# Attention in stages of a quarter of the queries, with maxima 29 units ahead instead of 40

## The reference

```
Q, K, V = (heads(WQ), heads(WK), heads(WV))
score = jnp.einsum('bhqd,bhkd->bhqk', Q, K) / jnp.sqrt(jnp.asarray(D_K, x.dtype))
score = score + mask
score = score - jnp.max(score, axis=-1, keepdims=True)
score = jnp.exp(score)
score = score / jnp.sum(score, axis=-1, keepdims=True)
out = jnp.einsum('bhqk,bhkd->bhqd', score, V)
```

## Time and profile before

| | us |
|---|---|
| median of 3 runs | 620.17 (620.04 to 621.65) |
| profiled execution | 619.71 |
| its span | 617.9 |
| PE busy | 571.0 (92%) |
| DVE busy | 475.7 (77%) |
| ACT busy | 330.8 (54%) |
| POOL busy | 191.1 (31%) |

### The profile page before, as it was taken

The page is one execution under the profiler, slowest core; times in us unless marked ns, Lnnn a source line. Parts: engine busy times, 40 slices in busy tenths (PEclk is TensorE's granted clock), DMA queues, the critical chain, the costliest instruction groups (busy, mean ns, idle before and its releaser), DMA issues.

```text
span 617.9 us, 11935 instructions
## 1 busy us (share of the span) xinstructions
PE 571.0 (92%) x3875; PEld 353.1 (57%) x3902; DVE 475.7 (77%) x1307; ACT 330.8 (54%) x602; POOL 191.1 (31%) x221
## 2 busy tenths in 40 slices
PE   2878999999999999999999988988899999999996
PEld 1433544444454534999999953444446666656554
DVE  6799889999989898455555579657689899976465
ACT  2752667676777676655555468753232642262224
POOL 1450000000254452133333311000007686688400
PEclk9798899999999999999999999998899999999999
DMA  8945727060813271111111043124010322421322
GB/s 196 234 145 204 243 73 216 2 215 2 224 42 100 67 210 32 44 49 47 47 47 47 25 130 90 70 70 120 0 46 15 90 63 59 123 87 40 103 68 68
DMA packets 55611, 57.99 MB, mean 94 GB/s; under 512 B 8650, under 2 KB 39402, under 8 KB 55514
## 3 DMA queue, kind: packets, MB, share of 16 engines
q1 hardware_dynamic: 51242, 50.56, 29.2%
q0 software_dynamic: 4320, 6.81, 3.5%
HBM read 41.96 MB, written 18.85 MB: 98 GB/s over the span
## 4 chain that ended last, share of the span: by engine, by line
PE 72%; DVE 17%; ACT 4%; issue 4%; DMA 1%; SPq 1%; ACTq 0%; DVEq 0%
PE banks L1690 11%; PE banks L1832 9%; PE banks L1963 7%; PE banks L1779 6%; PE banks L1757 6%; PE banks L1702 6%; DVE banks L1240 5%; PE banks L1952 5%; PE banks L1949 5%; PE banks L2014 4%; DVE mpart L1243 3%; ACT arena L809 2%; PE banks L1651 2%; PE banks L1760 2%; PE banks L1599 1%
## 5 line engine op out<-in xcount | busy, mean ns | idle before, releaser
L809 ACT ACTIVATE arena<-banks 128x512 f32<-128x512 f32 (+1 forms) x304 | 154.3, 583 | 75.2 <-PE banks L1760 40.7
L1240 DVE CUSTOM_DVE_ANT_0 banks<-banks,arena 128x512 f32<-128x512 f32 (+3 forms) x256 | 119.8, 511 | 9.3 <-PE banks L1779 8.4
L1779 PE MATMUL banks<-arena 96*128 96x512 bf16 (+3 forms) x384 | 113.5, 336 | 7.0 <-DVE mpart L1240 3.2
L1757 PE MATMUL banks<-arena 128*128 128x512 bf16 (+3 forms) x358 | 106.5, 327 | 3.9 <-ACT arena L809 3.3
L1243 DVE TENSOR_REDUCE mpart<-banks 128x1 f32<-128x512 f32 x128 | 85.8, 684 | 9.1 <-PE banks L1779 8.0
L1690 PE MATMUL banks<-arena 128*128 128x128 f32 x624 | 76.3, 275 | 1.0 <-ACT arena L743 1.0
L1690 PEld LDWEIGHTS banks<-arena 128*128 128x128 f32 x624 | 72.8, 192 | 1.5 <-ACT arena L743 1.5
L1832 PE MATMUL banks<-arena 128*9 128x512 f32 (+3 forms) x768 | 70.7, 487 | 0.0
L852 ACT ACTIVATE arena<-banks 125x512 f32<-125x512 f32 (+2 forms) x48 | 28.4, 595 | 71.2 <-PE banks L1949 46.2
L1757 PEld LDWEIGHTS banks<-arena 128*128 128x128 bf16 x384 | 37.8, 99 | 49.5 <-issue 23.6
L620 POOL DMA_INDIRECT results<-arena x39 | 37.7, 967 | 77.4 <-DVE arena L1134 77.4
(11 more groups left out here) (295 smaller groups left out, 868.3 us busy)
## 6 DMA issues: line engine op xcount, KB each, us to landing
k_parts<-arena SPq DMA_DIRECT2D x6, 768.0 KB, 7.4
arena<-in_L_ffn_experts_w_dram SPq DMA_DIRECT2D x2, 2048.0 KB, 11.0
arena<-results SPq DMA_DIRECT2D x8, 512.0 KB, 6.8
arena<-k_parts SPq DMA_DIRECT2D x7, 576.0 KB
arena<-q_parts SPq DMA_DIRECT2D x28, 144.0 KB
arena<-in_L_ffn_w_kernel_dram SPq DMA_DIRECT2D x8, 344.0 KB, 3.6
slots<-in_pad_rows_dram SPq DMA_DIRECT2D x1, 2535.0 KB, 12.1
arena<-slots SPq DMA_DIRECT2D x39, 65.0 KB, 1.8
```

The lines of the kernel that those rows point to most:

```text
L809: act.activation(Pr[:, r % 4, heads[0]:heads[-1] + 1, 0:n], ring_e[e % 3][:, 0:len(heads) * n].rearrange("p (j c) -> p j c", j=len(heads)) ...
L1240: ins = dve.tensor_tensor_reduce(unmasked, unmasked, tail_mask[:, 512 - n:512], 1.0, -BIG, ALU.add, ALU.max, part[:, at:at + 1])
L1757: ins = pe.matmul(ring_e[e % 3][:, at * n:at * n + n], QK[:, slot, j, 1, P * kt:P * kt + P], QK[:, slot, j, 0, q:q + n], start=True, stop= ...
L1779: ins = pe.matmul(ps[:, at * n:at * n + n], QK[0:TALL, slot, j, 0, P * i:P * i + P], QK[0:TALL, slot, j, 1, 512 * half:512 * half + n], st ...
```

## The change

- Stages are now a quarter of the queries (256) and one key tile: 20 stages and 36 exponential units a group. `Pr` holds eight narrow stages instead of four wide ones.
- Value matmuls come in six bursts of two to four stages. There are four "evac" copies a group, each of 256 columns.
- Maxima are finished by quarter: four "negmax" and four turns a group. Tiles go in the order (1, 0), (3, 2), (5, 4), (7, 6). Row (g, c) is now the row of quarter c. A turn is two matmuls instead of four, with 128 standing columns instead of 12; the buffer `MP` is wider for it and is filled with zeros at the start.
- 12 units come before the first exponential, then two for each exponential until the lead is 29 units, then 38 for 36 exponentials.
- The experts come at stage 4 of group 6. 225 exponential units and 266 maxima units then stand ahead of them, where it was 239 and 279; 63 and 38 stand behind, where it was 65 and 25.
- SyncE's list follows the plan: each row where its turn stands, loads for the group after next behind a group's fourth row. The vectors, the expert blocks and now also the experts' results are at the experts' step, so ahead of row (6, 3). The second sequence's parts are stored behind row (0, 2) instead of (0, 0).
- On ScalarE two copies of K and Q parts move from ahead of the first exponential to ahead of the fifth.

```diff
-STAGES = [(half, kt) for half in range(2) for kt in range(QT // 2 * half + QT // 2)]
+QW, NQ = 256, 4
+STAGES = [(c, kt) for c in range(NQ) for kt in range(2 * c + 2)]
 NS = len(STAGES)
+LAST_STAGE = [2, 6, 12, 20]
+BURSTS = {4: (0, 1), 7: (2, 3, 4, 5), 10: (6, 7, 8), 13: (9, 10, 11), 17: (12, 13, 14, 15)}
...
-SCATTER_AT, SCATTER_EVERY = 3 * EXP_UNITS + 20, 3
-EXPERTS_AT = (6, 3)
+SCATTER_AT, SCATTER_EVERY = 3 * EXP_UNITS + 14, 3
+EXPERTS_AT = (6, 4)
...
-MAX_TILES = ((3, 0, 2, 1), (7, 4, 6, 5))
-OPENING, LEAD, ROW_DELAY, POOL_DELAY = 22, 40, 3, 6
+MAX_TILES = ((1, 0), (3, 2), (5, 4), (7, 6))
+MAX_UNITS = sum(len(max_steps(0, i)) for i in range(QT))
+OPENING, LEAD, ROW_DELAY, POOL_DELAY = 12, 29, 3, 6
+ON_VECTOR = ((0, 0), (0, 1))
+PARTS_AT = 4
...
-            for i in MAX_TILES[half]:
+        for c in range(NQ):
+            for i in MAX_TILES[c]:
                 for step in max_steps(g, i):
                     count(step)
-            steps.append(("negmax", g, half))
-            due.append([ROW_DELAY if g + half == 0 else POOL_DELAY, ("maxrow", g, half)])
+            steps.append(("negmax", g, c))
+            due.append([ROW_DELAY if (g, c) in ON_VECTOR else POOL_DELAY, ("maxrow", g, c)])
...
-                plan += maxima(OPENING + (LEAD + half0 - OPENING) * n // half0 if n < half0 else n + LEAD)
+                plan += maxima(min(OPENING + 2 * n, LEAD + n * MAX_UNITS // EXP_UNITS))
...
+    if r == 1:
+        return [("pv", k - 1, stage) for stage in range(NS - 4, NS)] + [("evac", k - 1, NQ - 1)] if k > 0 else []
+    if k == NG or r not in BURSTS:
         return []
-    if r == 1:
-        return [("pv", k - 1, NS - 2), ("pv", k - 1, NS - 1), ("evac", k - 1, 1)] if k > 0 else []
-    if k == NG:
-        return []
-    return [("pv", k, r - 3), ("pv", k, r - 2)] + ([("evac", k, 0)] if r - 2 == QT // 2 - 1 else [])
+    steps = [("pv", k, stage) for stage in BURSTS[r]]
+    return steps + [("evac", k, c) for c in range(NQ) if LAST_STAGE[c] == BURSTS[r][-1] + 1]
...
-        Pr = region(12288, 8192).rearrange("p (s j t) -> p s j t", s=4, j=HG)
+        Pr = region(12288, 8192).rearrange("p (s j t) -> p s j t", s=8, j=HG)
...
-        MP = region(24832, 2 * QT * 3 * HG // 2, BF16).rearrange("p (s i c) -> p s i c", s=2, i=QT)
+        MP = region(24832, 1024, BF16).rearrange("p (s i c) -> p s i c", s=2, i=QT)
...
-            for g in range(NG):
-
-                if g == EXPERTS_AT[0] + 1:
+            def blocks_and_vectors():
...
-                if g == 0:
-                    sp.wait_ge(Z["rows_in"], 16 * 9)
-                for half in range(2):
-                    sp.wait_ge(Z["mrow_ready"], 2 * g + half + 1)
-                    sp.dma_start(QK[TALL:TALL + 3, g % 3, :, 0, 512 * half:512 * half + 512],
-                                 mrow[0:3 * HG, g % 2, 512 * half:512 * half + 512]).then_inc(mrow_in[half], 16)
-                    if (g, half) == (EXPERTS_AT[0] + 1, 0):
-                        load_results()
-                    elif (g, half) == (0, 0):
-                        store_parts(1)
+                    load_results()
+
+            def rows_in_place(g, c):
+                sp.wait_ge(Z["mrow_ready"], NQ * g + c + 1)
+                sp.dma_start(QK[TALL:TALL + 3, g % 3, :, 0, QW * c:QW * c + QW],
+                             mrow[0:3 * HG, g % 2, QW * c:QW * c + QW]).then_inc(mrow_in[c], 16)
+
+            def loads_behind(g):
...
+            sp.wait_ge(Z["rows_in"], 16 * 9)
+            for k in range(-1, NG + 1):
+                for step in PLANS[k]:
+                    if step[0] == "maxrow":
+                        _, g, c = step
+                        rows_in_place(g, c)
+                        if (g, c) == (0, 2):
+                            store_parts(1)
+                        if c == NQ - 1:
+                            loads_behind(g)
+                    elif step[0] == "experts0":
+                        blocks_and_vectors()
...
+            pool.memset(MP, 0.0).then_inc(Z["mem_set"], 1)
...
+            def second_copies(c):
+                for v in (2 * c, 2 * c + 1):
+                    act.wait_ge(Z["r1_done"], v - 3)
+                    act.copy(parts1[v % 2][:, 1, 512 * (c - 2):512 * (c - 2) + 512], rem1[:, v - 4, :]).then_inc(Z["p2_done"], 1)
...
+                        if e == PARTS_AT:
+                            second_copies(3)
                         act.wait_ge(Z["e_ready"], e + 1)
-                        if r >= 4:
-                            act.wait_ge(Z["pv_done"], r - 3)
-                        act.activation(Pr[:, r % 4, heads[0]:heads[-1] + 1, 0:n],
+                        if r >= 8:
...
-                        pe.wait_ge(Z["mp_ready"], 2 * g + half + 1)
+                        _, g, c = step
+                        pe.wait_ge(Z["mp_ready"], NQ * g + c + 1)
+                        pe.wait_ge(Z["mem_set"], 2)
                         ps = unit_free()
-                        for i in range(4):
-                            ins = pe.matmul(ps[0:3 * HG, P * i:P * i + P], MP[:, g % 2, 4 * half + i, :], ident_b, start=True, stop=True)
+                        for i in range(2):
+                            ins = pe.matmul(ps[:, P * i:P * i + P], MP[:, g % 2, 2 * c + i, :], ident_b, start=True, stop=True)
                         ins.then_inc(Z["m_ready"], 1)
```

More of the change, by code:

```diff
@@ L65, in heads_of @@
     return tuple(range(HG)) if j == 0 else ()
-STAGES = [(half, kt) for half in range(2) for kt in range(QT // 2 * half + QT // 2)]
+QW, NQ = 256, 4
+STAGES = [(c, kt) for c in range(NQ) for kt in range(2 * c + 2)]
 NS = len(STAGES)
+LAST_STAGE = [2, 6, 12, 20]
+BURSTS = {4: (0, 1), 7: (2, 3, 4, 5), 10: (6, 7, 8), 13: (9, 10, 11), 17: (12, 13, 14, 15)}
 def exp_steps(stage):
-    half, kt = STAGES[stage]
-    heads = [heads_of(j, 512 - max(0, P * kt - 512 * half)) for j in range(HG)]
+    c, kt = STAGES[stage]
+    heads = [heads_of(j, QW - max(0, P * kt - QW * c)) for j in range(HG)]
     return [("exp", stage, h) for h in heads if h]
@@ L375, in build @@
         Z = {n: sem(n) for n in names.split()}
-        mrow_in = [sem(f"mrow_in{i}") for i in range(2)]
+        mrow_in = [sem(f"mrow_in{i}") for i in range(NQ)]
         ld_x = [sem(f"ld_x{i}") for i in range(2)]
@@ L651, in _ @@
                             moved += 1
-                    elif step[0] == "negmax" and step[1:] != (0, 0):
+                    elif step[0] == "negmax" and step[1:] not in ON_VECTOR:
                         negated(*step[1:])
@@ L734, in _ @@
                 values_copy(c, banks[:, 0, :])
[L735 to L737 removed]
+                if c == 2:
+                    second_copies(c)
             def x_copy(c, j):
@@ L794, in _ @@
                 for step in PLANS[k]:
-                    if step[0] == "maxrow" and step[1:] != (0, 0):
-                        _, g, half = step
+                    if step[0] == "maxrow" and step[1:] not in ON_VECTOR:
+                        _, g, c = step
                         unit = UNIT_OF[step]
@@ L816, in _ @@
                     elif step[0] == "evac":
-                        _, g, half = step
-                        act.wait_ge(Z["pv_done"], NS * g + (NS if half else QT // 2))
+                        _, g, c = step
+                        act.wait_ge(Z["pv_done"], NS * g + LAST_STAGE[c])
                         if g >= 1:
-                            act.wait_ge(Z["m_ready"], UNIT_OF[("turn", g - 1, half)] + 1)
-                        act.copy(OT[:, 512 * half:512 * half + 512], O).then_inc(Z["o_evac"], 1)
+                            act.wait_ge(Z["m_ready"], UNIT_OF[("turn", g - 1, c // 2)] + 1)
+                        act.copy(OT[:, QW * c:QW * c + QW], O[:, 0:QW]).then_inc(Z["o_evac"], 1)
                     elif step[0] == "experts0":
```

73 lines of the change are left out of this document (35 added, 38 removed).

## The result

The changed kernel takes 647.51 us (median of 6 runs, 643.95 to 649.33) against 620.23 us: ratio 1.043, 95% interval 1.040 to 1.046. Forecast were 620.7 us and a range of 613.5 to 626.5, so it lies 21 us above the range. The profiled execution has a span of 647.5 us (before 617.9), 29.6 us more; it is the slowest of the six (649.33 us), so the stages add up to 2.3 us more than the 27.3 us between the medians.

The account below looks back on a forecast made before the run. PE or DVE was taken to set the pace, changing by stretch. -9.6 us up to the experts and +10.1 behind them gave +0.5 on 619.71, 620.2; the median's 0.46 more made 620.7 us, range 613.5 to 626.5.

Parts of the forecast that it names:

- Steady groups, 28.8 us: Groups of four heads without routing steps, bound by PE: from 29.05 to 28.8 us each.
- (c): Rival: narrow score matmuls cost more than their columns, 0.05 us each, 13 us for 256, 633 us in all; chance 0.04.
- (b): Rival: late rows in the opening, at (1,0) and (6,3) stop PE; sum +5 us, 625 to 626; chance 0.26.
- Turns, -0.38 us a group: Turns of the maxima on PE: 128 standing columns remove 0.19 us lost twice a group, 3.0 us over all groups.
- The opening, "unit 44 comes at about the same time": Start, where DVE sets the pace: maxima unit 44 only 0.3 us later, with 16 exponentials issued instead of 9.
- Row (1,0), 2.5 us: Group 1's first row, queued on SyncE behind group 2's loads: PE waits 2.5 us for it, bounds 0 and 4.
- Start of the experts, -0.8: SyncE sends the first expert block earlier, so PE's 0.9 us wait for it goes: -0.8 us.
- Row (6,3), 3.7 us: Behind the experts: this row queues behind the loads of the results, PE waits 3.7 us, DVE 3.2.
- Behind the experts, 62 us from the experts' end: Experts' end to last value matmul: 62 instead of 52.4 us, with 38 maxima units left instead of 25; +10.1 us.
- The tail, 0: From the last value matmul to the kernel's end: no change in time.
- (a): Rival: the maxima put off behind the experts are hidden; end there +3.5 instead of +10.1, about 614 us; chance 0.26.

Follow-up runs that it names:

- e1: Changed kernel with a lead of 40 units instead of 29, nothing else: 9.7 us faster than the changed kernel.
- e4: Changed kernel with the turns of the maxima standing 12 columns instead of 128: 647.57 us, no difference.
- e7: Kernel before with the turns of the maxima standing 128 columns instead of 12: 0.4% slower (1 to 4 us).
- e2: Changed kernel with GpSimd's subtractions waiting for DVE's first small chain: median 2.3 us lower, ratio to the kernel before still 1.043.
- e8: Kernel before without GpSimd's wait for DVE's first small chain between its two halves of work: median 624.76 us.
- e5: Changed kernel with the edits of e1 and e2 together: 1.1 us below e1 by medians, 0.4 by ratios.
- e6: e5 with the first exponential behind 22 units instead of 12, and ScalarE's last copies ahead of it: 4.4 us faster than e5, 2.2% over the kernel before.
- e3: Changed kernel with SyncE sending row (6,3) ahead of the results and x1: 6.0 us faster by the medians, 4 by the ratios.
- e15: e13 with the edits of e2 and e3 added; first full exponential behind the experts to last value matmul 64.9 us (changed kernel 71.5).
- e13: Changed kernel, the 38 units behind the experts moved ahead of the normalising; first full exponential there to last value matmul 64.9 us (changed kernel 71.5).
- e12: Kernel before with its lead growing from 40 to 48 ahead of the experts: 3.9 us lost ahead of them, stretch behind 51.8 instead of 51.6.
- e9: e6 with SyncE sending the vectors and first expert blocks behind row (6,3): PE's wait for the first block 3.9 instead of 5.0 us, nothing gained.

## Why the prediction was wrong, point by point

1. *Steady groups, 28.8 us.* Near: 29.1 where nothing else interferes. Its sum for five groups, 147.3 us (two at 30.45, three at 28.8), is what e1 does (147.7). Narrow matmuls cost what their columns cost; rival (c) is out. At the lead of 29 the groups take 3.7 us more: in groups 3 and 5 they are 2.0 us longer, with late rows for which PE waits 0.9 and 0.6 us, rival (b)'s mechanism where the prediction had not looked; in groups 1 and 2 it wasn't split up.
2. *Turns, -0.38 us a group.* Right at the turn (0.19 us each, e4), worth 0.2 us a group in halves (e7), nothing in quarters. The prediction called the load of 12 columns the slow one; it isn't slow, it starts late.
3. *The opening, "unit 44 comes at about the same time".* This step failed: 74.4 us instead of 63.9. I counted DVE's units and took their pace as given. The chain that moved forward was priced at its duration of before, without looking at what GpSimd did at its new place: 4.1 us at unit 4 (e2, e8). And the early exponentials stop PE, with the maxima behind them, in front of rows (1.4 us in the kernel after, 3.3 in e5). Of the 10.5 us at unit 44, e5 gets 2.0 back and e6, without the early exponentials, 9.2. From there to the experts the forecast held in sum: group 1 begins 12.5 us late (92.5 instead of 80.0 us), and the place is 13.4 us late. The clock wasn't a cause up to 64 us (0.80, and 0.78 before); from 64 to 81 it was lower (0.90 against full).
4. *Row (1,0), 2.5 us.* Didn't occur: PE came to its user at 92.5 us instead of 80.0 and waited for no row there.
5. *Start of the experts, -0.8.* It was +2.4: PE waits 1.3 us for ScalarE, and its first 16 matmuls take 3.65 us at half clock, where 2.05 were usual.
6. *Row (6,3), 3.7 us.* It waited 2.9. But the row's price was 4.7 by the time of `norm` and 5.7 in all (e3): PE had half clock for 3.5 us behind the wait, and the prediction had no term for the clock.
7. *Behind the experts, 62 us from the experts' end.* This step failed too, and most: 71.5 us from the first full exponential to the last value matmul, where the forecast comes to 61.6. DVE's work was sized about right, 40.5 us busy up to its last unit (forecast 38.9). Its idle time wasn't: 9.9 us, where the prediction took 1.5 "as before", 0.6 at the start and 3.2 for the row. Of the 9.9, 8.9 are waits for PE: 3.0 at the row, more in the half clock behind it, and the rest where PE and DVE stop each other over the ring. `finish` and `norm` were added up, but not put into the plan's order, where 8 units stand behind the first `norm`; the ring is four deep, so DVE's blocks of 4.6 and 2.0 us become waits of PE (2.75 and 2.35 us) and then of DVE. That table of the plan (units left when each block comes) could have been made before. By e3 and e15 this order alone is worth only 0.9 us. From DVE's last unit to the last value matmul it then takes 21.1 us instead of some 17.5: PE is 1 us ahead of DVE and not 2.4, and its last 27 exponentials take 22.0 us instead of 19.5. Even e13, which has the order that the sum assumed and no wait for the row, takes 64.9 us, where the forecast less the row is about 58; 6.8 us of it are at half clock, and the rest stays open.
8. *The tail, 0.* It was +2.6 in this trace; the only difference that the rows show is the clock.

The rivals: (b) had the right sign, and late rows are a good part of the loss, but it priced them at 5 us, and it had neither the slow chain nor the units and the clock behind the experts. (a) fell: 11 of the 13 units put off cost 9 us there and weren't hidden, though below some 25 of them units cost nothing more (e12).

## What to carry over

When an in-order plan is shifted, lay the plan's other blocks over the new positions and ask for each small step what now runs beside it and what stands ahead of it; sums of busy time don't show either, and the idle time of before can't be carried over. A producer's lead has no one price per unit: here units behind the experts cost nothing up to some 25, and 11 more than 27 cost 9 us, half clock included. Moving work ahead can also move a transfer behind another: the longer lead mended the row behind the experts and made the first expert block late. A row sent late cost more than its wait, since PE's clock was down behind it.

## What the runs showed of the hardware

- Small DVE operations (8 or 16 columns) beside GpSimd's 128x512 subtractions took 0.65 to 1.12 us instead of 0.2, each ending within 0.1 us of the end of a GpSimd instruction; a DVE reduction of one input beside them took 0.17.
- Loads of 12 standing columns took 0.09 us (of 128 columns 0.10), but in e4 each of 19 turns had the load engine idle just before, 0.28 us on average (kernel after, 128 columns: one of 19).
- Behind a wait of 2.9 us PE had 1.2 GHz for 3.5 us, and a 512-column matmul took 0.63 instead of 0.38 us in the record.
- The tail, the same instructions in all kernels, took 206.8 to 207.3 us where the mean granted clock over its first 48.7 us was 0.93 (before, e3, e12, e13, e15), 208.4 to 208.9 at 0.89, 209.7 to 210.0 at 0.86 (after, e2, e4, e7, e8, e9). That is one trace of each kernel, and the runs of the kernel before alone spread from 617.7 to 623.7 us, so which of the three a trace has can't be laid to an edit (e7: a turn, e8: a wait at 40 us). The kernel before has:

```profile
411.30:430.00 18.70, 14.35 (x67) 9.29 (x68) 10.34 (x44) 7.29 (x12) 0.34 (x2) 0.93 0.54 156
430.00:460.00 30.00, 26.87 (x74) 12.03 (x72) 23.20 (x49) 8.38 (x13) 0.98 (x2) 0.93 0.04 13
```

Against e7's rows above, PE has the same work; why it gets 1.2 GHz for longer there isn't settled. A comparison of two single traces of this kernel is uncertain by up to 3 us for that alone.
